# Two expert rings of a fused transformer kernel: their last tile in two halves, the sums by banks, the store in three parts

## What is computed

```python
h = _layernorm(x, axis=-1) * (1 + cb) + sb
x = x + gb * _L0_ffn_ref(h, ...)   # layer 0: 8 experts of 128 hidden channels and a shared one
...
for e in range(E):
    h = jax.nn.silu(rin @ w1[e].T) * (rin @ w3[e].T)
    out_sorted = out_sorted + m * (h @ w2[e].T)
...
x = x + gb * _L1_ffn_ref(h, ...)   # layer 1: 8 experts of 176 and a shared one
for e in range(E):
    expert_out = jax.nn.silu(xf @ w1[e]) @ w2[e]
    routed = routed + comb[:, e:e + 1] * expert_out
```

## Time and profile before

| | us |
|---|---|
| median of 3 runs | 1035.81 (1035.78 to 1039.97) |
| the profiled execution's own time | 1037.5 |
| its span, first to last instruction | 1035.6 |
| PE busy | 888.5 (86%) |
| DVE busy | 864.6 (83%) |
| ACT busy | 612.4 (59%) |
| POOL busy | 486.6 (47%) |
| mean granted clock of TensorE | 0.948 |

### The profile page before, as it was taken

One profiled execution on the slowest core, in us unless ns is written; L12 is line 12 of the kernel. 1 busy time (PEld: TensorE's weight loads), 2 busy tenths in 40 slices (PEclk: granted clock), 3 DMA queues, 4 the chain that ended last, 5 costly groups with the idle time before them and its releaser, 6 DMA issues. The chain is left out here.

```text
span 1035.6 us, 16928 instructions
## 1 busy us (share of the span) xinstructions
PE 888.5 (86%) x5375; PEld 601.1 (58%) x5454; DVE 864.6 (83%) x1849; ACT 612.4 (59%) x1327; POOL 486.6 (47%) x463
## 2 busy tenths in 40 slices
PE   5778999999999999999988996988847868767996
PEld 4456767766776677777766772545532243353554
DVE  6878999999999999997989978766989998785453
ACT  3758777777777777777766752222628728532111
POOL 2237657766776455545444456222283404216332
PEclk9979999999999999999999998999969989957999
DMA  6113333334433321232222141001000000030001
GB/s 244 33 55 105 129 125 127 108 128 129 128 107 128 98 82 62 82 127 90 86 62 87 62 148 58 1 2 31 10 22 1 0 3 0 1 138 1 1 1 41
DMA packets 44607, 73.50 MB, mean 71 GB/s; under 512 B 4658, under 2 KB 21042, under 8 KB 43880
## 3 DMA queue, kind: packets, MB, share of 16 engines
q1 hardware_dynamic: 35304, 59.84, 18.3%
q10 hardware_dynamic: 9216, 12.59, 3.3%
HBM read 57.86 MB, written 13.76 MB: 69 GB/s over the span
## 5 line engine op out<-in xcount | busy, mean ns | idle before, releaser
L502 PE MATMUL bank<-hTs,wA 128*128 128x512 bf16 x711 | 167.5, 381 | 3.9 <-DVE u L1711 0.7
L2308 POOL TENSOR_TENSOR xbuf<-xbuf,dec 128x384 f32<-128x384 f32 x64 | 53.4, 834 | 209.1 <-ACT xbuf L1183 173.2
L1711 DVE SCALAR_TENSOR_TENSOR u<-bank,chn,u 128x511 f32<-128x511 f32 (+2 forms) x192 | 142.9, 744 | 3.5
L502 PEld LDWEIGHTS bank<-hTs,wA 128*128 128x128 bf16 x768 | 75.1, 98 | 82.8 <-issue 3.9
L574 PE MATMUL bank<-wB,yb 128*128 128x256 f32 x512 | 121.2, 380 | 0.7 <-DVE acc L1667 0.7
L2376 POOL TENSOR_TENSOR hfl<-hf 128x512 bf16<-128x512 f32 x44 | 46.0, 1045 | 121.1 <-DVE hf L1970 67.2
L574 PEld LDWEIGHTS bank<-wB,yb 128*128 128x128 f32 x512 | 92.5, 190 | 11.1 <-issue 1.1
L502 PE MATMUL bank<-hTs,w13s 128*128 128x512 bf16 x354 | 88.6, 397 | 8.6 <-DVE uc L1959 4.0
L653 PE MATMUL bank<-Mm,xbuf 128*128 128x128 f32 x512 | 71.1, 282 | 22.9 <-DVE yv L1738 21.6
L2318 POOL TENSOR_TENSOR yb<-yv,gs 128x512 f32<-128x512 f32 x64 | 81.6, 1276 | 19.0 <-DVE yv L1738 18.8
L653 PEld LDWEIGHTS bank<-Mm,xbuf 128*128 128x128 f32 x512 | 64.6, 193 | 35.9 <-issue 27.3
(11 more groups left out here) (267 smaller groups left out, 2070.4 us busy)
## 6 DMA issues: line engine op xcount, KB each, us to landing
csb<-csd SPq DMA_DIRECT2D x64, 256.0 KB, 3.5
wA<-in_win SPq DMA_DIRECT2D x32, 256.0 KB, 4.3
wAd<-wA ACTq DMA_DIRECT2D x32, 256.0 KB, 4.4
wA<-wAd SPq DMA_DIRECT2D x32, 256.0 KB, 3.8
wB<-in_wob SPq DMA_DIRECT2D x8, 512.0 KB, 6.0
wBd<-wB ACTq DMA_DIRECT2D x32, 128.0 KB, 4.4
wB<-wBd SPq DMA_DIRECT2D x8, 512.0 KB, 5.3
CB<-in_wbc SPq DMA_DIRECT2D x2, 1024.0 KB, 9.4
```

The source lines that it names most:

```text
L502: last = nc.tensor.matmul(out, wpart(a, kt), hpart(c, kt), start=n == 0, stop=n == 5)
L1711: nc.vector.scalar_tensor_tensor(out=u[:, n % 2, d:S], in0=bank[0][:, 0:S - d], scalar=chn[:, hid, 3 - d:4 - d], in1=u[:, n % 2, d:S], op0 ...
```

## The change

The last tile of each ring (`m == B * nf - 1`) is worked off in two halves of 256 tokens by VectorE, GpSimd and TensorE: `words(m)` gives the halves, `fh_done`, `fhs_done` and `fout` count two for it. TensorE waits for the second half of `hfl` only before token group 2, and counts `fout` after group 1 (bank 6) and group 3 (bank 7). All later counts of these semaphores are one higher in ring 1 (`+ L`). `add_experts` works bank by bank, in all four places: multiply bank 6, add 512 columns, multiply bank 7, add 512 columns; `xf_done` counts two for a batch. Behind the last tile each bank's multiply waits for its own count. The store is three DMAs: batch 0, then the two halves of batch 1, each after its own count. The diff, without the lines that only change a count:

```diff
             def store():
-                sp.dma_start(io["out"].rearrange("(t p) d -> p t d", p=P), x_sb[:]).then_inc(q["d_out"], 16)
-                sp.wait_ge(q["d_out"], 16)
+                rows = io["out"].rearrange("(t p) d -> p t d", p=P)
+                for n, (t0, t1) in enumerate(((0, TB), (TB, TB + 2), (TB + 2, NT))):
+                    sp.wait_ge(q["xf_done"], 2 * B + 2 + n)
+                    sp.dma_start(rows[:, t0:t1], x_sb[:, t0:t1]).then_inc(q["d_out"], 16)
+                sp.wait_ge(q["d_out"], 48)
...
-                    pe.wait_ge(q["fhs_done"], number(f, b) + 1)
+                    n = number(f, b) + L
                     for t in range(TB):
+                        if t == 0 or m == B * nf - 1 and t == 2:
+                            pe.wait_ge(q["fhs_done"], n + 1 + t // 2)
                         for a, c in ((0, 0), (0, 1), (1, 0)):
...
-                    last.then_inc(q["fout"], 1)
+                        if t == TB - 1 or m == B * nf - 1 and t == 1:
+                            last.then_inc(q["fout"], 1)
...
+                def words(m):
+
+                    return (slice(0, S // 2), slice(S // 2, S)) if m == B * nf - 1 else (slice(0, S),)
...
-                        nc.vector.scalar_tensor_tensor(out=fg[:], in0=fth[:, par, :], scalar=1.0, in1=b0,
-                                                       op0=ALU.add, op1=ALU.mult).then_inc(q["fg_done"], 1)
-                        since("fout", n - 2 if m > 2 else 0)
-                        dve.wait_ge(q["fg_done"], n + 1)
-                        nc.vector.scalar_tensor_tensor(out=hf[:, m % 3, :], in0=fg[:], scalar=0.5, in1=b2,
-                                                       op0=ALU.mult, op1=ALU.mult).then_inc(q["fa_done"], 1)
-                        dve.wait_ge(q["fa_done"], n + 1)
-                        dve.sem_inc(q["fh_done"], 1)
+                        for k, w in enumerate(words(m)):
+                            nc.vector.scalar_tensor_tensor(out=fg[:, w], in0=fth[:, par, w], scalar=1.0, in1=b0[:, w],
+                                                           op0=ALU.add, op1=ALU.mult).then_inc(q["fg_done"], 1)
+                            since("fout", n - 1 if m > 2 else 0)
+                            dve.wait_ge(q["fg_done"], n + 2 + k)
+                            nc.vector.scalar_tensor_tensor(out=hf[:, m % 3, w], in0=fg[:, w], scalar=0.5, in1=b2[:, w],
+                                                           op0=ALU.mult, op1=ALU.mult).then_inc(q["fa_done"], 1)
+                            dve.wait_ge(q["fa_done"], n + 1 + k)
+                            dve.sem_inc(q["fh_done"], 1)
...
                 def add_experts(b):
 
-                    dve.wait_ge(q["fout"], base + nf * (b + 1))
+                    done = base + nf * (b + 1) + L
                     for m in range(2):
-                        last = nc.vector.tensor_tensor(xo[:, 2 * m:2 * m + 2, :],
-                                                       bank[6 + m][:, :].rearrange("p (t d) -> p t d", t=2),
-                                                       gm[:, L, 1, b, :].unsqueeze(1).to_broadcast([P, 2, D]), ALU.mult)
-                    link(last)
-                    part = slice(b * TB, (b + 1) * TB)
-                    nc.vector.tensor_tensor(x_sb[:, part, :], x_sb[:, part, :], xo[:], ALU.add).then_inc(q["xf_done"], 1)
-                    dve.wait_ge(q["xf_done"], L * B + b + 1)
+                        dve.wait_ge(q["fout"], done + m if b == B - 1 else done)
+                        link(nc.vector.tensor_tensor(xo[:, 2 * m:2 * m + 2, :],
+                                                     bank[6 + m][:, :].rearrange("p (t d) -> p t d", t=2),
+                                                     gm[:, L, 1, b, :].unsqueeze(1).to_broadcast([P, 2, D]), ALU.mult))
+                        part = slice(b * TB + 2 * m, b * TB + 2 * m + 2)
+                        nc.vector.tensor_tensor(x_sb[:, part, :], x_sb[:, part, :], xo[:, 2 * m:2 * m + 2, :], ALU.add)\
+                            .then_inc(q["xf_done"], 1)
+                    dve.wait_ge(q["xf_done"], 2 * (L * B + b + 1))
...
-                    nc.gpsimd.tensor_tensor(hfl[:, m % 3, :], hf[:, m % 3, :], hfh[:, m % 3, :], ALU.subtract)\
-                        .then_inc(q["fhs_done"], 1)
+                    for k in range(halves):
+                        pool.wait_ge(q["fh_done"], n + 1 + k)
+                        w = slice(S // halves * k, S // halves * (k + 1))
+                        nc.gpsimd.tensor_tensor(hfl[:, m % 3, w], hf[:, m % 3, w], hfh[:, m % 3, w], ALU.subtract)\
+                            .then_inc(q["fhs_done"], 1)
```

More of the change, by code:

```diff
@@ L908, in heads @@
                 keys_queries(0)
-                pe.wait_ge(q["xf_done"], B)
+                pe.wait_ge(q["xf_done"], 2 * B)
                 for half in range(2):
@@ L1965, in hidden @@
                         dve.wait_ge(q["fa_done"], n + 1)
-                        nc.vector.scalar_tensor_tensor(out=fg[:], in0=fth[:, par, :], scalar=1.0, in1=ua[:, par, :],
-                                                       op0=ALU.add, op1=ALU.mult).then_inc(q["fg_done"], 1)
-                        since("fout", n - 2 if m > 2 else 0)
-                        dve.wait_ge(q["fg_done"], n + 1)
-                        nc.vector.tensor_tensor(hf[:, m % 3, :], fg[:], uc[:, par, :], ALU.mult)\
-                            .then_inc(q["fh_done"], 1)
+                        for k, w in enumerate(words(m)):
+                            nc.vector.scalar_tensor_tensor(out=fg[:, w], in0=fth[:, par, w], scalar=1.0, in1=ua[:, par, w],
+                                                           op0=ALU.add, op1=ALU.mult).then_inc(q["fg_done"], 1)
+                            since("fout", n - 2 if m > 2 else 0)
+                            dve.wait_ge(q["fg_done"], n + 1 + k)
+                            nc.vector.tensor_tensor(hf[:, m % 3, w], fg[:, w], uc[:, par, w], ALU.mult)\
+                                .then_inc(q["fh_done"], 1)
@@ L1972, in hidden @@
                     else:
-                        since("fh_done", n)
+                        since("fh_done", n + 1)
                         dve.wait_ge(q["fth_done"], n + 1)
-                        nc.vector.scalar_tensor_tensor(out=fg[:], in0=fth[:, par, :], scalar=1.0, in1=b0,
-                                                       op0=ALU.add, op1=ALU.mult).then_inc(q["fg_done"], 1)
-                        since("fout", n - 2 if m > 2 else 0)
-                        dve.wait_ge(q["fg_done"], n + 1)
@@ L2371, in low_halves @@
                 for m in range(B * FT[L]):
-                    n = B * base + m
-                    pool.wait_ge(q["fh_done"], n + 1)
+                    n = B * base + m + L
+                    halves = 2 if m == B * FT[L] - 1 else 1
                     if m > 2:
                         pool.wait_ge(q["fout"], n - 2)
-                    nc.gpsimd.tensor_tensor(hfl[:, m % 3, :], hf[:, m % 3, :], hfh[:, m % 3, :], ALU.subtract)\
-                        .then_inc(q["fhs_done"], 1)
+                    for k in range(halves):
[3 more added lines that the diff above has]
+                            .then_inc(q["fhs_done"], 1)
             def heads():
```

5 lines of the change are left out of this document (2 added, 3 removed).

## The result

The changed kernel takes 1034.22 us (median of 20 runs, 1030.26 to 1040.23); the kernel before, on the same chip, 1039.61 us (20 runs, 1035.78 to 1043.45). The ratio on record is 0.996, 95% interval 0.9943 to 0.9976: 0.4% faster. The profiled execution took 1035.04 us, its span 1033.2 us where the earlier trace rows has 1035.6.

A forecast was written before the change was run, and what follows sets the result against it. The prediction saw a serial, uncovered chain from ring 1's last tile through the final store. Its terms -1.39 - 2.1 + 0.87 - 0.4 = -3.0 us took the median from 1035.8 to 1032.8 us, range 1029.9 to 1035.8.

The forecast's parts named there:

- Ring 1's chain: Ring 1's last tile in halves, sums by banks: the last store is issued 1.39 us sooner.
- The store: Kernel's end: store cut in three, so only a 256 KB landing of 2.3 us is seen; -2.1 us.
- the third rival: Kernel's end: last 256 KB store takes 6.5 us to land, store part +2.1, time 1037.0 us; chance 0.07.
- The boundaries: Between batches in both rings: split sums lengthen TensorE's wait, first add held by GpSimd; +0.52 and +0.35, together +0.87 us.
- Ring 0's end: Ring 0's last tile in halves: TensorE goes on sooner despite a VectorE-GpSimd collision; -0.4 us.
- The second term: Ring 0's end: VectorE's own work is done 1.5 us sooner, gaining nothing while the keys are late.
- The first rival: Ring 0's end: TensorE's clock stays high, worth about 2.6 to 3.0 us, time 1030.2 us; chance 0.15.
- The second rival: Ring 1's boundary: longer wait lowers TensorE's clock, losing 1.7 us, time 1034.5 us; chance 0.10.
- The fourth: Halving the tile brings nothing because VectorE waits on its halves; -1.39 becomes 0, time 1034.2 us; chance 0.10.

The follow-up runs named there:

- half_ring1: Changed kernel with only ring 1's last tile halved, ring 0's left whole; 1036.57 us, ratio 0.997 to the kernel before.
- rel_filled: Changed kernel, boundary multiplies before adds, zeroing released by the multiplies, nine unused matmuls in ring 0's last-tile wait; 1025.32 us, ratio 0.9892 to the kernel before.
- mults_first: Changed kernel with both multiplies of a batch boundary before both adds; 1031.77 us, ratio 0.9936 to the kernel before.
- after: The changed kernel itself, with all edits of the change against the kernel before; 1034.22 us, ratio 0.996.
- before_filled: Kernel before plus thirteen unused matmuls in TensorE's wait for ring 0's last tile; 1037.59 us, ratio 1.0006 to the kernel before.
- filled_end: Changed kernel plus nine unused matmuls in TensorE's wait for ring 0's last tile; 1034.53 us, ratio 0.9969 to the kernel before.
- after_again: The changed kernel measured a second time, nothing altered; 1033.78 us, ratio 0.9963 to the kernel before.
- no_halves: Changed kernel with both last tiles whole, sums by banks and three stores kept; 1038.12 us, ratio 0.9998 to the kernel before.
- released: Changed kernel with boundary multiplies before adds and each bank's zeroing released by its multiply, not the adds; 1026.74 us, ratio 0.99 to the kernel before.
- released_whole: Kernel before with each bank's zeroing at the boundaries released by its multiply; whole tiles, one add, one store; 1032.94 us, ratio 0.9953 to the kernel before.

## Why the prediction was right, step by step

**Size and sign.** Forecast: 3.0 us, 0.29%. Measured: 0.4% and 0.37%, intervals 0.13 to 0.62% together. The time given, 1032.8 us, was taken off a median of 1035.81 that three runs had shown; twenty gave 1039.61 for the same kernel. The kernel before lay lower in those three than it does in general, and the forecast came out 1.4 us below the measured median although it promised less gain than was had. That the time fell in the range is luck in part: the base was 3.8 us too low and the gain 2.4 us too small by the medians, and the two offset each other. Off the median of twenty runs the same -3.0 would have given 1036.6 us. A level taken from three runs carries the 6 us of scatter of the stretch ahead of A.

**Ring 1's chain, -1.39: right, -1.36**, with two errors that stayed hidden. The second `fg` was to start 0.15 us behind the first `hf`; it waited 0.50 us, as its row above says. Why is open. It isn't the wait for `hf` and the increment of `fh_done` that stand between the two: at the boundary `xo` follows `hf` through the same two in 0.14 us (989.72 + 0.69 to 990.55), and in half_ring1, with the same instructions, the second `fg` starts 0.15 us behind, as forecast:

```profile
1027.59 0.42 DVE L1991 SCALAR_TENSOR_TENSOR hf<-fg,bank 128x256 f32<-128x256 f32 x1
1028.16 0.42 DVE L1987 SCALAR_TENSOR_TENSOR fg<-fth,bank 128x256 f32<-128x256 f32 x1
```

GpSimd started 0.20 us behind `hf` for 0.13, and took 0.61 us for a half where 0.66 was forecast. So TensorE's second six began 3.20 us after the first `fg`, forecast 2.97. Neither shows at the end, because VectorE's four sums were what is late, as the prediction said: they began 2.76 us after it, forecast 2.74. half_ring1 shows that the wait costs nothing: F - E is 5.50 us there too.

**The store, -2.1: mechanism right, size -2.35.** 256 KB land in 2.1 us, forecast 2.3, in every kernel with three stores but rel_filled (median 3.3 of its two, span's end 3.68 us after F). So the slow landing of the third rival exists in a small form: once in nine profiles, worth 1.1 us, not the 4.2 us that it was priced at. The sequence 256 KB 2.1, 512 KB 2.9, 1024 KB 4.4 is a straight line within 0.1 us: 1.35 us fixed and 3.0 us per MB. The estimate from the Trainium skill ("DMA: Bandwidth & Descriptors", section Anatomy of one DMA), 2.6 us for 256 KB, was half a microsecond too long; its 4.4 us for 1 MiB agrees. The page fits that formula to DMAs issued by GpSimd, and these stores are issued by SyncE.

**The boundaries, +0.52 and +0.35: right, +0.60 and +0.41.** The first add ends 0.54 us after the subtraction (686.42 to 686.96), as the earlier trace rows had it; the rest of 0.07 is that the subtraction began 0.23 us behind the first multiply in ring 0 and 0.05 behind in ring 1, where the earlier trace rows had 0.16 and a step before it. That VectorE's add with both inputs in SBUF waits for GpSimd is also what the Trainium skill says ("SBUF — State Buffer", SBUF: two separate sides); mults_first shows it by the order alone. What the prediction didn't see is that this wait need not be there: the banks that TensorE zeroes had been read 1.3 us before the add's end, the first of them earlier still. Nor did it see that the low clock behind ring 0's boundary, which stood in its rows (0.51), hung on the length of this wait: 1.7 us.

**Ring 0's end, -0.4: direction right, size wrong.** With the clock low in both profiles it was -0.74. With the clock at 1.00 in both it is 9.50 - 8.36 = -1.14. The failed step is the time at which TensorE leaves the tile, "could go on to the next stage at 722.05" for "leave it at 722.43". The next stage begins with these rows, of the kernel before and then of after:

```profile
722.65 1.91 PE L441 MATMUL bank<-cst,acc 128*128 128x128 f32 x8
```

```profile
723.15 1.92 PE L443 MATMUL bank<-cst,acc 128*128 128x128 f32 x8
```

Counted from the first `fg` it is 4.28 us and 3.46 us, so TensorE goes on 0.82 us sooner, not 0.38. Before, 722.43 was the start of the last matmul, 0.22 us early as a time of leaving; and in the halves the second six began 2.78 us after the first `fg`, forecast 3.02. In this profile 0.32 of the 0.74 us are lost again from C to D.

The second term is VectorE: the prediction wrote that its own work is done 1.5 us sooner, "which gains nothing while the keys are late". At the low clock that holds, since VectorE waits for the keys in both kernels (1.65 and 2.48 us). At the high clock it fails. The keys on ScalarE and VectorE's copy of them, of before_filled and then of filled_end:

```profile
729.35 0.60 ACT L1347 ACTIVATE ks<-bank 128x512 f32<-128x512 f32 x1 [2.14 <-PE bank L844]
730.52 0.42 DVE L2030 COPY acc<-ks 128x512 f32<-128x512 f32 x1
```

```profile
730.75 0.60 ACT L1352 ACTIVATE ks<-bank 128x512 f32<-128x512 f32 x1 [2.14 <-PE bank L849]
731.38 0.43 DVE L2042 COPY acc<-ks 128x512 f32<-128x512 f32 x1
```

In before_filled the keys are ready 8.93 us after the first `fg` and lie for 0.57 us, because VectorE is still busy with its own work; in filled_end they are ready at 8.33 and are taken 0.03 us later. So 0.60 of the 1.14 us are the keys, which TensorE brings sooner, and the other 0.54 are VectorE's own work, the term put at nothing.

**The first rival, clock high at ring 0's end, 0.15: it did happen**, in five of the six profiles of kernels that halve this tile and have no filler, and not in after's. The prediction's ground against it, "the total idleness hardly shrinks", was no ground: with 2.3 us of idleness and a short second pause in place of 3.18 us the clock stayed in after_again and fell in after. Its price was 2.6 to 3.0 us; the rows give 10.76 - 8.36 = 2.4. Whether the median got it is open: the differences of the medians (5.4 and 3.8 us) lie between the -3.1 of one profile's ledger and the -6.1 of the other's, which a mixture of both levels would give.

**The second rival, clock falls in ring 1:** it didn't, in any profile; 2.41 us of idleness were not enough there (window 993.60:998.00 above, 1.00). **The fourth, halving void:** no_halves against after, 1.62 us, excludes it.

## What to carry to other kernels

When an engine waits at a boundary, read the wait's releaser and ask which instruction really frees what it needs: here one wait moved from the add to the multiply gave 4.6 us, more than halving tiles, splitting sums and cutting the store gave for sure (2.7). At a kernel's end cut the last tile and the last store, since nothing covers either; in the middle, split sums only if none of the pieces with both inputs in SBUF meets GpSimd. And cut profiles at fixed events: columns that repeat to 0.02 us carry a verdict which a median with 6 us of scatter can't.

## What the runs showed of the hardware

- The clock behind an idle stretch of TensorE fell each time in ring 0's boundary after 2.56 to 3.16 us (nine profiles) and never after 0.70 us (four); in ring 1 it read 1.00 behind 2.0 to 2.7 us (nine profiles). At ring 0's end 2.3 us, and a second pause of 0.08 us between the halves, left it high in one profile of the changed kernel and low in another.
- Time won beside a higher clock in one place can be lost in another: before_filled gained 2.0 us by C and had lost 1.85 of it by D, most of it in 15 us in which the granted clock read 0.70 for 0.88, in code that it shares with the kernel before.
- An add of 512 columns takes 0.69 us alone and 0.92, 1.09 or 1.20 us when it starts 0.67, 0.49 or 0.39 us after a GpSimd subtraction of 1.04 us: each ended 0.54 to 0.55 us after that one's end. Its order against two reads of PSUM decides whether it is paid.
- The stretch at the lower clock behind ring 0's boundary costs 1.68 us, the same in released against after and in released_whole against before; ring 1, where it is missing, gains exactly the earlier start of `rows_out` (1.89 and 1.47 us).
- The second `fg` of ring 1's last tile starts 0.50 to 0.52 us behind the first `hf` in the eight kernels that halve both rings' last tiles and 0.15 us in half_ring1, with the same instructions. The cause is open.
